# Deformable convolution with a routed expert FFN: expert results added onto an early-written output by the indirect DMA

## The chip, the cores and the metric

The kernel runs on one core of one Trainium2 chip. The metric is the device time of one execution in microseconds (us). The engines are PE (matmul), DVE (vector), ACT (activation), POOL (GpSimd), and SP, which issues most of the DMAs. Each engine has its own instruction queue, worked off in order, and they meet only at semaphores.

## The reference

The input is a batch of 4 images of 32x32 positions with 128 channels, 4,096 rows in all, in float32.

```python
x = x + conv(_ln_c(x), w_offset, b_offset, filt)      # 3x3 deformable convolution
t = _to_tokens(x)                                     # x1: 4,096 rows of 128
t = t + ffn(_ln_t(t), gate_w, gate_b, W1, b1, W2, b2)

# ffn, on rows xf
probs = softmax(xf @ gate_w + gate_b)                 # 8 experts
top2_vals, top2_idx = top_k(probs, 2)
cw = zeros.at[rows, top2_idx].add(top2_vals)
for e in range(8):
    y = gelu(xf @ W1[e] + b1[e]) @ W2[e] + b2[e]      # hidden width 256
    out = out + cw[:, e] * y
```

So every row goes through two of the eight experts, and its output is x1 plus the two results, each times its softmax share.

## The kernel before

**Bands.** The 4,096 rows are 32 bands of 128. The `step` functions of the engines run once per band in a loop of four bands per turn (`band_loop`, L305). Band b takes its sampling weights on PE (`spread_hats`, L1274), DVE (`multiply`, L918) and ACT (`copy_y`, L725), samples its window (`sample`, L1307, three groups), has ACT copy the samples out of PSUM (`evacuate_samples`, L755), and projects them with the filter (`project`, L1321). DVE then adds the projection to x1 (`residual`, L926), takes mean and variance, ACT takes the square root (`std_band`, L763) between the first and the second sample copy of the next band, and DVE takes the reciprocal and normalises (`normalise`, L941). PE computes the gate, DVE picks the two experts (`choose`, L955) and the row's place in each expert's region (`place_rows`, L985, four links). POOL packs the normalised row with its destination number (`pack`, L584) and scatters it with two indirect DMAs per band into the DRAM table `routed` (`scatter`, L596). `project` of a band waits for `place_rows` link 0 and for the sample copies; ACT's order of work within a band is fixed by its `step` (L790), DVE's by its own (L1093).

**Plan.** After the last band DVE counts the blocks of 256 rows per expert and writes a table `blk_i` of 39 blocks, in the order of experts (L1145 to L1168). SP and ACT fill the ends of the regions with padding rows. Blocks that are not needed (idle blocks, at the end of the 39) read a region of padding.

**Blocks.** Each of the 39 blocks uses one of four slots. SP reads the block's first row from `blk_i` into registers, copies the expert's weights (W1, b1, W2, b2) from the SBUF tensor `w_all` into the slot's `w_blk` (`load_weights`, L486), and loads 256 rows (`load_rows`, L492). PE transposes the rows, multiplies by W1, ACT applies Gelu, PE multiplies by W2 (`down`, L1437), DVE adds b2 (`finish`, L1194), and POOL writes the result rows with two indirect DMAs (`send`, L652) into the DRAM table `result`, a row's place there being its own number for its first expert and 4,096 further on for its second. Padding rows are dropped by the bounds check. DVE does not reuse a slot's `y` or `to` before the sends of the block four before have landed.

**Combination.** When all sends have landed (SP, L527), SP reads `result` back in groups of four bands, ACT multiplies one of the two results by its share (L846 to L852), DVE multiplies the other, adds x1 and adds both (L1213 to L1224), and SP stores the output. The shares are computed in one go after the plan (L1171 to L1180).

```python
652  def send(turn, place):
654      pool.wait_ge(s.y_done, i + 1)
655      pool.wait_ge(s.to_ready, i + 1)
657      for j in range(SUBS):
658          nc.gpsimd.indirect_dma_start(result, ..., y[:, slot, j, :], None, bounds_check=...)
```

Of the kernel before, what the change touches and what calls it, by code (L numbers as in the profile page):

```python
# [20 lines left out]
F32 = mybir.dt.float32  # L21
# [7 lines left out]
P = 128  # L29
# [18 lines left out]
ZERO_ROWS = 40  # L48
# [17 lines left out]
assert IDLE + BLOCK <= REGION  # L66
BLOCKS = (2 * P * BANDS + EXPERTS * (BLOCK - 1)) // BLOCK
ROW = C + 1

W_UP = HID + HALVES  # L70
WROW = W_UP + HALVES * C + C
RING = 4
SP_PADS = EXPERTS // 2
GB = 4
BACK = 4
# [13 lines left out]
def window_constants():  # L89
# [28 lines left out]
    for b in range(BANDS):  # L118
# [10 lines left out]
    token = np.arange(BANDS)[None, :, None] * P + p[:, None, None]  # L129
    dest = (token + np.arange(2) * (P * BANDS)).astype(np.int32)  # L130
    padding = np.zeros((P, SUBS, ROW), np.int32)
    padding[:, :, C] = 2 * P * BANDS + np.arange(SUBS) * P + p[:, None]
# [9 lines left out]
        "padding": padding,  # L142
    }


def program(nc, x_rows, x_tiles, w_offset, b_offset, filt, gate_w, gate_b, experts,
            rel, spread, fold, base, ident, before, table, dest, padding, out):
    with ExitStack() as ctx:
# [11 lines left out]
        result = nc.dram_tensor("result", [2 * P * BANDS + BLOCK, C], F32, kind="Internal").ap()  # L160
# [12 lines left out]
        dest_sb = sb("dest_sb", [P, BANDS, 2], I32)  # L173
# [20 lines left out]
        top_all = sb("top_all", [P, BANDS, EXPERTS])  # L194
# [23 lines left out]
        rs1 = sb("rs1", [P, 2])  # L218
        xn2 = sb("xn2", [P, 2, C])
# [30 lines left out]
        e_all = sb("e_all", [P, BANDS, EXPERTS])  # L250
        e_sum = sb("e_sum", [P, BANDS])
        share = sb("share", [P, 2, BANDS])
# [8 lines left out]
        blk_first = sb("blk_first", [1, BLOCKS])  # L261
        blk_row = sb("blk_row", [1, BLOCKS])
        blk_i = sb("blk_i", [1, BLOCKS], I32)
        pad_row = sb("pad_row", [1, EXPERTS], I32)


        w_blk = sb("w_blk", [P, RING, WROW])
# [5 lines left out]
        y_back = wide[:, 0:BACK * 2 * GB * C].rearrange("p (r c2 b c) -> p r c2 b c", r=BACK, c2=2, b=GB)  # L273
        res = sb("res", [P, BACK, GB, C])

# [4 lines left out]
        for name in (  # L280
# [7 lines left out]
            "route stashed place_psum place_ready placed_ready slot_f_ready slot_ready payload_ready scat_even scat_odd "  # L288
            "exp_in exp_out warmed share_step count_psum plan_step pad_ready plan_ready idle_written pads_written "
            "rows_in_0 rows_in_1 rows_in_2 rows_in_3 w_in_0 w_in_1 w_in_2 w_in_3 "  # L290
            "rowsT_psum rowsT_ready h_psum h_ready y_psum2 to_ready y_done "
            "sent_0 sent_1 sent_2 sent_3 back_0 back_1 back_2 back_3 scaled res_step res_ready "
            "stored_0 stored_1 stored_2 stored_3"
# [58 lines left out]
        back_arrived = (s.back_0, s.back_1, s.back_2, s.back_3)  # L352
        stored = (s.stored_0, s.stored_1, s.stored_2, s.stored_3)
# [26 lines left out]
        def _(sp):  # L380
# [75 lines left out]
            sp.dma_start(routed[IDLE_ROW:IDLE_ROW + BLOCK, :].rearrange("(j p) w -> p j w", p=P),  # L456
                         padding_sb[:, :, :].bitcast(F32)).then_inc(s.idle_written, 16)
# [4 lines left out]
            with sp.If(flag):  # L462
                pad_image()
                with sp.Fori(0, BANDS) as b:
                    sp.wait_ge(s.base_free, b + 1)
                    sp.dma_start(base_sb[:, :], base[b]).then_inc(s.base_loaded, 16)
            with sp.Else():
                for b in range(2, BPI):
                    load_windows(b, b % 2, 0, TILE * b)
                with sp.Fori(1, IMAGES) as m:  # L470
                    for r in range(BPI):
                        load_windows(m * BPI + r, r % 2, m, TILE * r)

# [5 lines left out]
            def first_rows(turn, place, n):  # L479
# [3 lines left out]
                    min_val=0, max_val=IDLE_ROW)  # L483
                return rows

            def load_weights(turn, place, row):  # L486
                i, slot, uses = block_at(turn, place)
                expert = nc.s_assert_within(row >> REGION_BITS, 0, EXPERTS - 1)
                at_least(sp, s.y_done, i - (RING - 1))
# [20 lines left out]
            sp.wait_ge(s.plan_ready, 1)  # L510
# [15 lines left out]
            for slot in range(RING):  # L526
                sp.wait_ge(sent[slot], 16 * SUBS * (TURNS + (slot < REST)))  # L527
            back = result[0:2 * P * BANDS, :].rearrange("(c g b p) d -> c g p b d", c=2, b=GB, p=P)
            out_v = out.rearrange("(g b) p c -> g p b c", b=GB)

            def load_back(g):
                for c2 in range(2):
                    sp.dma_start(y_back[:, g % BACK, c2], back[c2, g]).then_inc(back_arrived[g % BACK], 16)

            for g in range(BACK):
                load_back(g)
            for g in range(BANDS // GB):
                sp.wait_ge(s.res_ready, g + 1)
                sp.dma_start(out_v[g], res[:, g % BACK, :, :]).then_inc(stored[g % BACK], 16)
                if g + BACK < BANDS // GB:  # L540
                    load_back(g + BACK)
            for slot in range(BACK):
                sp.wait_ge(stored[slot], 16 * (BANDS // GB // BACK))
# [3 lines left out]
        def _(pool):  # L547
# [10 lines left out]

            pool.wait_ge(s.early_loaded, 16 * N_EARLY)
# [937 lines left out]
```

## Time and profile before

| what | us |
|---|---|
| three runs | 402.12, 403.15, 404.54 |
| median | 403.15 |
| span of the profiled execution | 400.06 |
| median less span | 3.1 |
| PE busy, share of the span | 315.2, 79% |
| POOL busy | 228.9, 57% |
| DVE busy | 227.3, 57% |
| ACT busy | 195.6, 49% |

The profile gives the span of its execution, from the first instruction to the last; its time around the span is not measured by itself, so the difference to the median stands for it. Busy shares are means over stages with different limits, so the stages have to be read one by one: 0 to 45 us the first normalisation and the offsets, 45 to 250 the bands, 250 to 274 the plan and the first loads, 274 to 375 the blocks, 375 to 400 the combination. L numbers are lines of the kernel before. An entry such as "[0.88 <-DVE slot L1007]" is the engine's idle time before the instruction and what ended it. SPq, ACTq, POOLq and DVEq are the engines' queues with their register, wait and DMA-issuing instructions.

### The profile page before, as it was taken

The numbers are of one execution on the slowest core, as the hardware profiler recorded it, in microseconds if no ns is written. First come the engines' busy times: TensorE is split into PE (matmuls) and PEld (weight loads), VectorE is DVE, ScalarE is ACT, GpSimd is POOL, SyncE is SP. The second block draws the span as 40 slices with busy tenths as digits, with TensorE's granted clock in tenths as the row PEclk, the third lists the DMA queues.
The fourth block names the chain that finished last, engine by engine and source line by source line (L and its number), as shares of the span: only waits on it lengthen the run. The fifth ranks groups of instructions, "written<-read, shape, count | busy, mean of one in ns | idle before, by whom it ended". The sixth has DMA issues, their size and how long they took to land.

```text
span 400.1 us, 9901 instructions
## 1 busy us (share of the span) xinstructions
PE 315.2 (79%) x2395; PEld 264.9 (66%) x2395; DVE 227.3 (57%) x988; ACT 195.6 (49%) x526; POOL 228.9 (57%) x351
## 2 busy tenths in 40 slices
PE   0999799999999999999999995049989797885000
PEld 0354688888889888898898994038867686774000
DVE  3983257878778787787887876502222122332085
ACT  1253566565565665756656652314444444442063
POOL 4013043777777777777777766204777777777300
PEclk9999899999999999999999999558999999999555
DMA  8958612222222222222222220855777777762298
GB/s 209 274 164 249 265 54 75 89 80 100 78 93 85 82 99 78 90 94 76 98 84 83 95 80 26 145 139 169 223 222 243 230 231 232 227 221 72 82 315 234
DMA packets 52450, 57.88 MB, mean 145 GB/s; under 512 B 6892, under 2 KB 40423, under 8 KB 52424
## 3 DMA queue, kind: packets, MB, share of 16 engines
q1 hardware_dynamic: 45031, 48.16, 39.1%
q0 software_dynamic: 4544, 8.44, 6.6%
q10 hardware_dynamic: 2848, 0.99, 1.4%
q8 instruction: 9, 0.15, 0.2%
q14 instruction: 18, 0.14, 0.1%
HBM read 30.70 MB, written 14.97 MB: 114 GB/s over the span
## 4 chain that ended last, share of the span: by engine, by line
PE 53%; SPq 16%; issue 10%; DMA 6%; ACT 4%; DVE 4%; POOL 2%; ACTq 2%; DVEq 1%; POOLq 0%
PE bank L1326 18%; PE bank L1315 15%; SPq L481 5%; PE bank L1248 5%; SPq L490 4%; SPq L496 3%; DMA wide<-result 2%; PE bank L1279 2%; PE bank L1433 2%; ACT samp L758 2%; PE bank L1269 2%; PE bank L1260 2%; POOL result L658 2%; DMA routed<-padding_sb 1%; DMA result<-y,to 1%
## 5 line engine op out<-in xcount | busy, mean ns | idle before, releaser
L658 POOL DMA_INDIRECT result<-y,to x78 | 76.8, 985 | 43.8 <-DVE to L1191 26.8
L1326 PE MATMUL bank<-filt_sb,samp 128*128 128x128 f32 x576 | 79.3, 283 | 4.1 <-ACT samp L758 2.5
L1326 PEld LDWEIGHTS bank<-filt_sb,samp 128*128 128x128 f32 x576 | 69.1, 191 | 18.1 <-ACT samp L758 14.2
L1315 PE MATMUL bank<-S,xwin 100*128 100x144 f32 x512 | 78.9, 298 | 1.8 <-issue 1.7
L602 POOL DMA_INDIRECT routed<-payload,slot x64 | 63.2, 987 | 18.5 <-issue 13.5
L758 ACT ACTIVATE samp<-bank 128x432 f32<-128x432 f32 (+1 forms) x96 | 46.3, 484 | 52.8 <-PE bank L1315 52.8
L1315 PEld LDWEIGHTS bank<-S,xwin 100*128 100x128 f32 x512 | 67.7, 193 | 2.2 <-issue 2.0
L923 DVE TENSOR_TENSOR S<-ysp,bank 100x512 f32<-100x512 f32 (+1 forms) x96 | 52.5, 550 | 22.9 <-ACT ysp L729 21.8
L1433 PE MATMUL bank<-rowsT,w_blk 128*128 128x256 f32 x156 | 44.4, 408 | 13.3 <-DMA w_blk<-w_all 10.2
L1199 DVE TENSOR_TENSOR y<-bank,w_blk 128x256 f32<-128x256 f32 x39 | 16.6, 425 | 66.0 <-PE bank L1442 64.2
L822 ACT ACTIVATE rowsT<-bank 128x256 f32<-128x256 f32 x39 | 15.0, 384 | 61.0 <-PE bank L1424 61.0
L729 ACT ACTIVATE ysp<-bank 100x512 f32<-100x512 f32 (+1 forms) x96 | 43.6, 494 | 2.4 <-PE bank L1279 1.5
L579 POOL TENSOR_TENSOR rest<-hat 128x180 f32<-128x180 f32 x32 | 17.0, 531 | 47.2 <-ACT hat L715 47.2
L1442 PE MATMUL bank<-w_blk,hid 128*128 128x128 f32 x312 | 42.1, 279 | 0.0
L1433 PEld LDWEIGHTS bank<-rowsT,w_blk 128*128 128x128 f32 x156 | 27.5, 197 | 20.0 <-ACT hid L829 8.0
L1442 PEld LDWEIGHTS bank<-w_blk,hid 128*128 128x128 f32 x312 | 38.8, 195 | 0.3 <-ACT hid L829 0.2
L829 ACT ACTIVATE hid<-bank,w_blk 128x256 f32<-128x256 f32 x78 | 32.6, 473 | 0.6 <-PE bank L1433 0.6
L1279 PE MATMUL bank<-hatT,spread_sb 120*100 120x512 bf16 (+1 forms) x96 | 32.0, 333 | 0.1
L1282 PE MATMUL bank<-hatT,spread_sb 120*100 120x512 bf16 (+1 forms) x96 | 31.2, 325 | 0.8 <-DVE S L923 0.8
L1424 PE MATMUL bank<-ident_sb,rows_in 128*128 128x128 f32 x78 | 15.9, 287 | 15.1 <-DMA rows_in<-routed 15.1
L570 POOL TENSOR_TENSOR dist<-offs,rel_sb 128x180 f32<-128x180 f32 x32 | 16.2, 508 | 19.3 <-issue 10.7
L1424 PEld LDWEIGHTS bank<-ident_sb,rows_in 128*128 128x128 f32 x78 | 11.0, 147 | 20.3 <-DMA rows_in<-routed 15.1
(110 smaller groups left out, 493.1 us busy)
## 6 DMA issues: line engine op xcount, KB each, us to landing
w_blk<-w_all SPq DMA_DIRECT2D x39, 321.0 KB
xwin<-lines SPq DMA_DIRECT2D x64, 120.0 KB
xwin<-lines SPq DMA_DIRECT2D x32, 160.0 KB
rows_in<-routed SPq DMA_DIRECT2D x39, 129.0 KB
wide<-result SPq DMA_DIRECT2D x16, 256.0 KB, 4.8
w_all<-in_experts SPq DMA_DIRECT2D x4, 642.0 KB, 7.4
out_tiles<-res SPq DMA_DIRECT2D x8, 256.0 KB, 4.6
wide<-in_x_rows SPq DMA_DIRECT2D x3, 512.0 KB, 8.6
```

Source lines behind the costliest of these rows:

```text
L602: nc.gpsimd.indirect_dma_start(routed, bass.IndirectOffsetOnAxis(slot[:, par, c2:c2 + 1], 0), payload[:, par, c2, :], None).then_inc((s.sc ...
L658: nc.gpsimd.indirect_dma_start(result, bass.IndirectOffsetOnAxis(to[:, slot, j:j + 1].bitcast(U32), 0), y[:, slot, j, :], None, bounds_che ...
L729: nc.scalar.activation(ysp[:, slot, 0:n], bank[slot][0:Q, 0:n], ACT.Copy).then_inc(s.y_ready, 1)
L758: nc.scalar.activation(sample_view(par, g), bank[5 + (par + g) % 2][:, 0:GROUPS[g] * TAPS * TT].rearrange("c (t k p) -> c t k p", k=TAPS, ...
L829: nc.scalar.activation(hid[:, slot, h, :], bank[RING + slot][:, h * BLOCK:(h + 1) * BLOCK], ACT.Gelu, bias=w_blk[:, slot, HID + h:HID + h ...
L923: nc.vector.tensor_tensor(S[:, par, c0:c0 + n], ysp[:, slot, 0:n], bank[2 + slot][0:Q, 0:n], ALU.mult).then_inc(s.S_ready, 1)
L1279: nc.tensor.matmul(bank[slot][0:Q, 0:n], spread_sb[:, 2 * odd, :], moving, start=True, stop=True).then_inc(s.y_psum, 1)
L1282: nc.tensor.matmul(bank[2 + slot][0:Q, 0:n], spread_sb[:, 2 * odd + 1, :], moving, start=True, stop=True).then_inc(s.x_psum, 1)
L1315: last = nc.tensor.matmul(bank[5 + (par + g) % 2][:, i * TAPS * TT:(i + 1) * TAPS * TT], xwin[:, par, t, :], weights[:, t], start=True, st ...
L1326: last = nc.tensor.matmul(bank[7][:, 0:C], samp[:, par, j, :], filt_sb[:, order[j], :], start=(j == 0), stop=(j == TAPS - 1))
L1433: last = nc.tensor.matmul(bank[RING + slot][:, h * BLOCK:(h + 1) * BLOCK], w_blk[:, slot, h * P:(h + 1) * P], rowsT[:, slot, :], start=Tru ...
L1442: last = nc.tensor.matmul(bank[slot][:, BLOCK + j * C:BLOCK + (j + 1) * C], hid[:, slot, h, j * P:(j + 1) * P], w_blk[:, slot, W_UP + h * ...
```

## The change

The table `result` and the combination are gone. The output tensor itself is the target of the sends, which add their rows to what lies there (an indirect DMA with an add). The output holds x1 before that: SP stores each band's x1 into it during the bands. A row's two results come from two experts, so POOL lets no block start before all blocks of earlier experts have landed. Results are scaled by their share before they are sent; the share travels with the row, computed per band, and rows grow from 129 to 130 words. Padding and idle blocks are added to spare rows of the output, which POOL zeroes at the start. The square root and reciprocal become Ln and Exp on ACT. W2 is no longer copied into the slot: PE reads it from `w_all` at an address from a register.

```diff
 # SP, per band
+            def begin_out(b):
+                at_least(sp, s.x1_ready, b + 1)
+                settle(sp)
+                sp.dma_start(out[bass.ds(b * P, P), :], x1[:, b, :]).then_inc(s.out_begun, 16)
-            sp.dma_start(routed[IDLE_ROW:IDLE_ROW + BLOCK, :].rearrange("(j p) w -> p j w", p=P),
-                         padding_sb[:, :, :].bitcast(F32)).then_inc(s.idle_written, 16)
+            sp.dma_start(routed[IDLE_ROW:LAST_ROW + BLOCK, :], idle.bitcast(F32)).then_inc(s.idle_written, 16)
 # SP, per block
-                sp.dma_start(w_blk[:, slot, :], w_all[:, expert, :]).then_inc(w_arrived[slot], 16)
+                sp.dma_start(w_blk[:, slot, :], w_all[:, expert, 0:W_KEPT]).then_inc(w_arrived[slot], 16)
             def load_rows(turn, place, row):
+                at_least(sp, s.y_done, (i - (RING - 1)) * SUBS)
 # POOL, at the start
+            for n in range(RING):
+                nc.gpsimd.dma_start(out[TRASH + n * part:TRASH + (n + 1) * part, :].rearrange(
+                    "(p r) c -> p (r c)", p=P), zero[:, 0:part * C // P]).then_inc(sent[n], 16)
 # POOL, per block
+            def send(turn, place, ahead):
+                for other in range(RING):
+                    pool.wait_ge(sent[other], ((ahead + (RING - 1 - other)) >> 2) * (16 * SUBS) + 16)
                 pool.wait_ge(s.to_ready, i + 1)
                 settle(pool)
                 for j in range(SUBS):
+                    pool.wait_ge(s.y_done, i * SUBS + (j + 1))
+                    settle(pool)
                     nc.gpsimd.indirect_dma_start(
-                        result, ..., y[:, slot, j, :], None, bounds_check=2 * P * BANDS - 1, oob_is_err=False
+                        out, ..., y[:, slot, j, :], None, compute_op=ALU.add).then_inc(sent[slot], 16)
 # ACT, per band
             def std_band(b, par):
                 act.wait_ge(s.mean1_ready, b + 1)
-                nc.scalar.activation(sd1[:, par:par + 1], mv1[:, par, 1:2], ACT.Sqrt,
-                                     bias=eps_t[:, :]).then_inc(s.std1_ready, 1)
+                nc.scalar.activation(sd1[:, par:par + 1], mv1[:, par, 1:2], ACT.Ln,
+                                     bias=eps_t[:, :]).then_inc(s.ln_ready, 1)
+                act.wait_ge(s.ln_ready, b + 1)
+                at_least(act, s.xn2_ready, b - 1)
+                nc.scalar.activation(rs1[:, par:par + 1], sd1[:, par:par + 1], ACT.Exp, scale=-0.5
+                                     ).then_inc(s.std1_ready, 1)
+            def exp_top(b, par):
+                act.wait_ge(s.ntop_ready, b + 1)
+                at_least(act, s.share_ready, b - 1)
+                nc.scalar.activation(e_top[:, par, :], top[:, par, :], ACT.Exp, bias=ntop[:, par:par + 1],
+                                     accum_out=e_sum[:, par:par + 1]).then_inc(s.e_ready, 1)
 # ACT step: exp_top(b - 3) between evacuate_tokens(b - 2) and copy_y(b, 2)
 # DVE, per band
-                nc.vector.reciprocal(rs1[:, par:par + 1], sd1[:, par:par + 1]).then_inc(s.dve_rstd, 1)
-                    nc.vector.tensor_copy(top_all[:, b, :], top[:, par, :]).then_inc(s.stashed, 1)
+                    nc.vector.tensor_scalar(ntop[:, par:par + 1], top[:, par, 0:1], -1.0, None, ALU.mult
+                                            ).then_inc(s.ntop_ready, 1)
+                elif link == 4:
+                    dve.wait_ge(s.e_ready, b + 1)
+                    nc.vector.reciprocal(e_inv[:, par:par + 1], e_sum[:, par:par + 1]).then_inc(s.inv_ready, 1)
+                else:
+                    dve.wait_ge(s.inv_ready, b + 1)
+                    nc.vector.tensor_scalar(payload[:, par, :, C + 1], e_top[:, par, 0:2], e_inv[:, par:par + 1], None,
+                                            ALU.mult).then_inc(s.share_ready, 1)
 # DVE step: link 4 of band b - 3 after residual(b - 1) link 0, link 5 after hats(b + 2) link 0
 # DVE, per block, after the addition of b2
+                dve.wait_ge(s.y_sum, i + 1)
+                for j in range(SUBS):
+                    nc.vector.tensor_scalar(y[:, slot, j, :], y[:, slot, j, :], rows_in[:, slot, j, C + 1:C + 2], None,
+                                            ALU.mult).then_inc(s.y_done, 1)
 # PE, per block
-                                                w_blk[:, slot, W_UP + h * C:W_UP + (h + 1) * C],
+                                                w_all[:, expert, W_KEPT + h * C:W_KEPT + (h + 1) * C],
...
 # removed: load_back, res, y_back, share and the three combination loops of SP, ACT and DVE
```

## Rows read from the trace of the kernel before

**Rows 1.** Busy time by stage: start:end, length, busy (instructions) per engine, clock, DMA.
```profile
core 0: us, PE busy (x) PEld busy (x) DVE busy (x) ACT busy (x) POOL busy (x), PEclk, DMA share, GB/s
58.00:238.00 180.00, 175.82 (x1465) 156.33 (x1464) 143.19 (x665) 110.50 (x291) 129.41 (x226) 1.00 0.26 87
274.00:375.00 101.00, 79.02 (x518) 68.56 (x516) 24.94 (x75) 40.98 (x110) 76.81 (x78) 0.97 0.64 200
```

**Rows 2.** Timeline of POOL, block stage (start, duration; first two and last of 78).
```profile
274.23 0.99 POOL L658 DMA_INDIRECT result<-y,to  x1 [20.37 <-DVE to L1191]
275.52 0.99 POOL L658 DMA_INDIRECT result<-y,to  x1 [0.30 <-DVE to L1191]
...
373.52 0.98 POOL L658 DMA_INDIRECT result<-y,to  x1 [0.30 <-issue]
```

**Rows 3.** The sends' line (durations min/median/max in ns), and waits of 265 to 376.
```profile
L658 POOL DMA_INDIRECT result<-y,to x78: 982/984/995, 274.2 to 373.5; - x78
...
DVE to L1191 <- DMA result<-y,to: 9.7, 20, 1.3
```

**Rows 4.** Chain that ended last (start, duration): two landings of sends, and the end.
```profile
360.63 3.35 DMA result<-y,to
...
373.52 2.12 DMA result<-y,to
...
396.58 0.69 DVE res L1223
```

**Rows 5.** Timeline at the end of the bands: a POOL queue that had run empty.
```profile
250.41 0.31 DVE L1007 CAST slot<-slot_f 128x2 uint32<-128x2 f32 x1
...
251.63 0.96 POOL L602 DMA_INDIRECT routed<-payload,slot  x1 [0.88 <-DVE slot L1007]
```

**Rows 6.** Timeline of one band, ACT with the two ends of its chain.
```profile
160.06 0.53 ACT L758 ACTIVATE samp<-bank 128x432 f32<-128x432 f32 x1 [1.64 <-PE bank L1315]
161.13 0.17 DVE L939 BATCH_NORM_AGGREGATE mv<-st 128x2 f32<-128x6 f32 x1
161.33 0.29 ACT L765 ACTIVATE sd<-mv,eps_t 128x1 f32<-128x1 f32 x1
161.53 0.51 ACT L758 ACTIVATE samp<-bank 128x432 f32<-128x432 f32 x1
162.19 0.40 ACT L758 ACTIVATE samp<-bank 128x288 f32<-128x288 f32 x1
```

**Rows 7.** Chain that ended last, two bands on.
```profile
162.64 1.38 PE bank L1326 x10
...
167.51 0.30 ACT sd L765
...
168.63 0.18 DVE place L991
...
168.89 1.38 PE bank L1326 x10
```

**Rows 8.** Waits in the bands, 58 to 238 (total, times, longest); SP's of the span.
```profile
POOL rest L579 <- ACT hat L715: 34.5, 28, 3.8
...
PEld bank L1326 <- ACT samp L758: 13.2, 23, 0.7
...
SPq L414 <- PE bank L1315: 103.1, 30, 4.7
```

**Rows 9.** SP's line of the weight copies in the block stage.
```profile
L490 SPq DMA_DIRECT2D w_blk<-w_all x39: 495/507/602, 257.6 to 358.7; - x39
```

**Rows 10.** Timeline of the first 20 us.
```profile
11.31 1.63 DVE L864 BATCH_NORM_STATS2 st<-wide 128x6 f32<-128x128 f32 x8
...
17.14 0.52 POOL L561 CAST spread_sb<-spread_f 120x400 bf16<-120x400 f32 x1 [12.49 <-DMA gb_sb<-in_gate_b]
```

**Rows 11.** Chain that ended last, between the bands and the blocks.
```profile
256.13 5.79 DMA routed<-padding_sb
262.17 2.27 DMA rows_in<-routed
```

More of the change, by code:

```diff
@@ L142, in window_constants @@
         "padding": padding,
+        "idle": idle,
     }
 def program(nc, x_rows, x_tiles, w_offset, b_offset, filt, gate_w, gate_b, experts,
-            rel, spread, fold, base, ident, before, table, dest, padding, out):
+            rel, spread, fold, base, ident, before, table, dest, padding, idle, out):
     with ExitStack() as ctx:
@@ L472, in _ @@
                         load_windows(m * BPI + r, r % 2, m, TILE * r)
+                        begin_out(m * BPI + (r - 3))
+                for b in range(BANDS - 3, BANDS):
+                    begin_out(b)
             sp.wait_ge(s.pad_ready, 1)
@@ L526, in _ @@
             for slot in range(RING):
[L527 to L543, printed above, removed]
+                sp.wait_ge(sent[slot], 16 + 16 * SUBS * (TURNS + (slot < REST)))
         @block.gpsimd
@@ L650, in _, with blocks_ahead @@
                 scatter(BANDS - 1, 1)
-            def send(turn, place):
+            pool.wait_ge(s.plan_ready, 2)
+            pool.wait_ge(s.out_begun, 16 * BANDS)
+            for n in range(RING):
+                pool.wait_ge(sent[n], 16)
+            def blocks_ahead(turn, place, n):
+                _, values = nc.values_load_multi_w_load_instructions(
+                    blk_ahead[0:1, bass.ds(turn * RING + place, n)], engines=[mybir.EngineType.Pool],
+                    min_val=0, max_val=BLOCKS)
+                return values
+            def send(turn, place, ahead):
                 i, slot, uses = block_at(turn, place)
-                pool.wait_ge(s.y_done, i + 1)
+                for other in range(RING):
+                    pool.wait_ge(sent[other], ((ahead + (RING - 1 - other)) >> 2) * (16 * SUBS) + 16)
                 pool.wait_ge(s.to_ready, i + 1)
@@ L796, in step @@
                         evacuate_tokens(b - 2, par)
+                    if not known or b >= 3:
+                        exp_top(b - 3, 1 - par)
                     if not known or b >= 1:
@@ L1187, in keep_dest @@
                     settle(dve)
[L1188 removed]
+                sent_before(slot, uses)
                 if not isinstance(i, int):
@@ L1435, in up, with experts_of, down @@
                 last.then_inc(s.h_psum, 1)
-            def down(turn, place):
+            def experts_of(first, n):
+                _, rows = nc.values_load_multi_w_load_instructions(
+                    blk_i[0:1, bass.ds(first, n)], engines=[mybir.EngineType.PE],
+                    min_val=0, max_val=LAST_ROW)
+                return [nc.s_assert_within(row >> REGION_BITS, 0, EXPERTS - 1) for row in rows]
+            def down(turn, place, expert):
                 i, slot, uses = block_at(turn, place)
```

209 lines of the change are left out of this document (103 added, 106 removed).

## The prediction

> **What bounds the kernel now.** I read busy time by stage first, then the timeline of the engine that looks saturated in each stage, then the chain that ended last.
>
> Blocks: POOL is 76.8 us busy in 101 us, PE 79.0 [rows 1]. The shares hide who paces. POOL's timeline shows it: the 78 sends start every 1.29 us, 0.98 us each and 0.30 us apart, from 274.23 to 373.52 without one larger gap [rows 2], so the stage is 78 x 1.29 = 100.5 us of POOL. DVE confirms it: 20 times it waits 9.7 us in all for landed sends [rows 3]. SP comes close: its 39 weight copies go from 257.6 to 358.7 [rows 9], 2.66 us apart with the wait for the first rows among them, against POOL's 2.58 per block.
>
> Bands: PE is busy 175.8 of 180 us [rows 1], but busy here includes pipelined overlap. The next band's projection waits for ACT's last sample copy: 23 times, 13.2 us of weight-load idling [rows 8]. ACT's chain in one band runs without a hole: first sample copy at 160.06, square root at 161.33, second copy 161.53, last copy 162.19 [rows 6], projection at 162.64 [rows 7]. The square root begins as soon as DVE's variance is there (161.13 + 0.17 = 161.30 [rows 6]). Every fourth band goes by DVE instead: square root 167.51, `place` 168.63, projection 168.89 [rows 7]. So ACT and DVE set the band's period of about 6.2 us jointly with PE.
>
> Combination: the last send lands at 373.52 + 2.12 = 375.64 [rows 4], and the span ends at 400.06; 24.4 us are reading back, scaling, adding and storing.
>
> **The change part by part**, against the profiled span of 400.06 us; the median of the runs is 3.1 us above it, and I carry these along.
>
> *Combination removed.* 24.4 us go. SP still has to see the last sends land; 0.4 us for that is my estimate: 24.0 saved. The last sends belong to idle blocks. Today their rows are dropped, landing in 2.12 us; a send with rows takes 3.35 [rows 4]. They now carry rows: +1.2.
>
> *Sends.* The number stays 78. How long POOL takes for a send with an add no row shows. Nearest is the same instruction without it, 982 to 995 ns over all 78, the emptied ones included [rows 3]: POOL's time does not follow what leaves. I take no change. Ends: below, 78 x 0.03 us = 2 us gained, because the bounds check goes and a scatter without one takes 0.96 [rows 5]; above, half as much again, 78 x 0.49 = 38 us. The landing could grow by a read of the destination: 0 to 2.3 us, a row load's whole way [rows 11]; I take 0, since the sends land like a plain scatter in the nearest row.
>
> *New wait on earlier experts.* Seven times in 39 blocks the expert changes and POOL waits until everything sent has landed. The queue is in order: the next send, the register loads and everything behind stand still. From a send's start to its landing 3.35 us [rows 4]; from a released wait to the start of a send on an empty POOL queue 0.9 us (250.72 to 251.63 [rows 5]); less the 1.29 us pitch [rows 2], 3.0 us each. POOL is the bound, so nothing covers it: 7 x 3.0 = +21. Low end: restart hidden, 7 x 2.1 = 14; high end: a read leg added, 7 x 5.3 = 37. What waits behind POOL is DVE (`y`, `to`), then PE and SP, which all have the time. POOL's register work for the four waits lies beside its send, 0.98 us of each 1.29 [rows 2]; exposed, it would show as a longer pitch.
>
> *DVE's scaling* (two small operations per block after b2) lies beside POOL's pitch; DVE is 24.9 of 101 us busy [rows 1]. Only the first block pays it, about 0.4 us.
>
> *W2 in place, smaller copies, PE's register loads.* Weight copies shrink from 321 to 193 KB. Since POOL paces, I cost them at nothing either way; the cover is POOL's 2.58 us per block plus 21 us of stalls. If POOL were faster, SP [rows 9] would be next. The new wait in `load_rows` comes one place ahead of one that `load_weights` already had: nothing.
>
> *Bands, ACT.* `std_band` costs 0.20 us of ACT now (161.33 to 161.53 [rows 6]). Ln must finish (0.29), the wait releases (0.04), Exp takes another 0.20: 0.53, so +0.33 on the chain that releases the projection. `exp_top` stands before a hole of 1.64 us in which ACT waits for samples [rows 6]: hidden.
>
> *Bands, DVE.* Two small operations (links 4, 5), each with a wait, and a wait in `choose`, stand between the residual and the variance; the copy of `top` and `ntop` swap evenly. In a queue where such an operation takes 0.1 to 0.2 us, the variance comes about 0.2 us later, and Ln with it. The removed reciprocal lies behind Exp and shortens only the `place` path. Together 0.33 + 0.22 = 0.55 us on 31 bands: +17. Ends: 0, if PE's own work covers it (its idle is 4 us in 180 [rows 1]); and 1.0 per band, 31 us, if each wait costs 0.1 more.
>
> *Bands, the rest.* SP's store of x1 needs some 0.5 us of a queue that waits 103 us for samples [rows 8]; POOL's extra wait stands in a queue that waits 34.5 us for ACT [rows 8]. Nothing; without that cover SP would lose 0.5 us per band.
>
> *Start.* POOL zeroes 1 MB by four DMAs while the images load. DVE takes up the second image at 11.31 [rows 10]; a delay of that image would show there. POOL itself is idle until 17.14 [rows 10]. The larger idle table (0.9 MB) moves while the offsets are computed. +0.5, ends 0 and 3.
>
> *Between bands and blocks.* Two more links before the count, +0.4, the reciprocal of the last band, -0.2, the first scaling +0.4. The longer plan lies beside the padding rows, which land 5.79 us after their issue at 256.13 [rows 11]. +0.6.
>
> Sum: 400.06 - 24.0 + 1.2 + 21 + 17 + 0.5 + 0.6 = 416.4, with 3.1 around it **419.5 us**.
>
> **Rivals.**
>
> *The bands pay nothing (faster).* Place: ACT between the first and last sample copy. PE is 97.7% busy there; if its period is its own, the 0.55 us vanish under it, and the missing reciprocal may shorten the `place` bands (0.2 us in 8 bands, -1.6). Then 419.5 - 17 - 1.6 = 401, with 394 if the stalls are at their low end as well. It decides at a band period that stays at or below 6.2 us. Against it: the 13.2 us that PE's weight loads wait for ACT [rows 8], and the projection that follows the last copy at once.
>
> *The add costs POOL or the DMA engines more (slower).* Every send longer by up to 0.49 us: 438 at half of that, 457 in full. For it: nothing in this trace adds on the way. Against it: the emptied sends take POOL as long as full ones [rows 3]. The Trainium skill (Collectives: The Full Stack, Why ReduceScatter is half of AllGather) says that an add in the DMA engines needs two source reads, two read descriptors per chunk where a copy has one. No row shows it; by that rule this rival is the one that happens.
>
> *The tables do not stay (slower).* Were Ln and Exp to reload ACT's table each time, every band would pay over 2 us, some 480. The change asks for one set ahead of the bands; little speaks for it.
>
> **How the numbers follow.** The forecast case has 0.54, with a narrow own range of 408 to 430. The bands that pay nothing 0.2, the dearer add 0.22, the tables 0.04. A measurement of this kernel can tell about 0.5%, 401.1 to 405.2. Faster: 0.11 from the first rival and 0.06 from the forecast case with all its low ends together: 0.17. Same: 0.05 and 0.02: 0.07. Slower takes the rest, 0.76. The range goes from 397, between the low rival's ends, to 448, inside the dearer add; below it some 0.08 and above it some 0.11 are left.
>
> **What would show it.** The combination's 24 us gone, the last landing near the end. In POOL's timeline seven gaps of about 4.3 us between the starts of neighbouring sends, the rest still at 1.29. A band period of 6.7 instead of 6.2, with Ln and Exp 0.33 us apart and the variance later. I am wrong if the pitch of sends inside an expert is not 1.29, if the gaps are far from 3 us above it, or if the band period does not move.

## The result, and the profile after

The changed kernel takes 463.11 us (462.13 to 464.9, 4 runs) against 403.38 us (402.12 to 404.54, 4 runs): 1.149 times as long, 95% interval 1.146 to 1.153. The forecast was 419.5 with a range up to 448. The sign was right, the size was not. The profiled execution took 463.29 us with a span of 461.5, so the two spans, 400.06 and 461.5, differ by 61.4 us. The time around the span is 1.8 to 2.0 us in every execution whose span is on record; the 3.1 us that stood for it before the change is larger because the execution profiled there was shorter than the median. One execution of the kernel before, 1119.59 us beside f5 and f6, was a slow one and is left out below.

Windows of the changed kernel, the two stages of [rows 1] (bands, then blocks):

```profile
core 0: us, PE busy (x) PEld busy (x) DVE busy (x) ACT busy (x) POOL busy (x), PEclk, DMA share, GB/s
62.00:255.00 193.00, 179.39 (x1466) 158.10 (x1465) 145.17 (x692) 124.10 (x378) 131.16 (x227) 1.00 0.28 91
292.00:457.00 165.00, 100.64 (x521) 82.84 (x519) 41.34 (x151) 40.97 (x110) 121.14 (x78) 0.79 0.58 101
```

The blocks went from 101 to 165 us. POOL still issues 78 sends there, but they keep it busy for 121.14 us in place of 76.81. The sends' line, answering [rows 3] (ns, minimum, median, maximum; then what ended the idle time before them and who waited):

```profile
L679 POOL DMA_INDIRECT out_tiles<-y,to x78: 1544/1552/1610, 292.1 to 454.7; - x78
its engine sat idle before it (us, times) until:
  issue: 23.8, 51
...
  DVE to L1225: 52.7, 22
```

One send costs POOL 1.55 us with the add, 0.98 without. DVE, which waited 9.7 us for landed sends before, now waits 52.7: everything stands behind POOL. POOL's timeline, answering [rows 2]: the first sends, four of the seven restarts after a wait for earlier experts, and the last.

```profile
292.05 1.61 POOL L679 DMA_INDIRECT out_tiles<-y,to  x1 [20.39 <-DVE to L1225]
293.97 1.57 POOL L679 DMA_INDIRECT out_tiles<-y,to  x1 [0.30 <-issue]
...
305.77 1.55 POOL L679 DMA_INDIRECT out_tiles<-y,to  x1 [2.79 <-issue]
...
402.97 1.55 POOL L679 DMA_INDIRECT out_tiles<-y,to  x1 [3.65 <-DVE y L1237]
...
431.71 1.55 POOL L679 DMA_INDIRECT out_tiles<-y,to  x1 [3.06 <-DVE y L1237]
...
441.72 1.55 POOL L679 DMA_INDIRECT out_tiles<-y,to  x1 [2.89 <-DVE y L1237]
...
454.71 1.55 POOL L679 DMA_INDIRECT out_tiles<-y,to  x1 [0.30 <-issue]
```

Inside an expert the pitch is 1.857 us, of which 0.30 is the old gap. Seven gaps are larger: 2.79, 3.23, 3.18, 2.94, 3.65, 3.06, 2.89, together 19.6 us above seven ordinary ones. So the stage, from the first send's start to the last one's end, is 164.2 us against 100.3: 78 x 0.568 = 44.3 for the longer sends and 19.6 for the gaps make the 63.9.

The chain in one band, answering [rows 6]:

```profile
158.10 0.53 ACT L778 ACTIVATE samp<-bank 128x432 f32<-128x432 f32 x1 [1.64 <-PE bank L1337]
...
159.26 0.29 ACT L785 ACTIVATE sd<-mv,eps_t 128x1 f32<-128x1 f32 x1
159.59 0.20 ACT L789 ACTIVATE rs<-sd 128x1 f32<-128x1 f32 x1
159.69 0.51 ACT L778 ACTIVATE samp<-bank 128x432 f32<-128x432 f32 x1
...
160.35 0.40 ACT L778 ACTIVATE samp<-bank 128x288 f32<-128x288 f32 x1
```

Ln and Exp start 0.33 us apart. From Ln's start to the next sample copy it is 0.43 us, where the square root left 0.20. The two ends of the bands are the first and the last projection:

```profile
55.81 0.94 PE L1348 MATMUL bank<-filt_sb,samp 128*128 128x128 f32 x6 [1.56 <-ACT samp L778]
...
258.83 0.94 PE L1348 MATMUL bank<-filt_sb,samp 128*128 128x128 f32 x6
```

Before, these stood at 51.88 and 241.71. So the start lost 3.9 us and the 31 band periods 13.2 (203.02 against 189.83, or 0.43 each). Each is a difference of two profiles, and profiles scatter: the first projection lies between 51.88 and 54.09 in the five kernels here with the old start, and between 53.89 and 56.03 in the eleven with the new one; the 31 periods take 189.8 to 190.7 us in the four kernels whose bands are as before, and 202.8 to 204.5 in the eleven that have the changed bands. From the last projection to the first send it is 33.2 us against 32.5. After the last send's end 5.2 us are left against 25.55. What they wait for is on record in the drains, the last that each queue does before the engines meet at the end (in the kernel before, then in the changed one; ns, start in us):

```profile
L148 POOLq DRAIN  x1: 13807/13807/13807, 367.3 to 367.3; - x1
```

```profile
L153 POOLq DRAIN  x1: 12367/12367/12367, 448.9 to 448.9; - x1
L153 SPq COMPARE_BRANCH  x1: 38/38/38, 458.1 to 458.1; - x1
L153 SPq DRAIN  x1: 13/13/13, 458.3 to 458.3; - x1
```

SP has seen all sends land at 458.1 and is done at 458.3, but POOL's drain ends only at 461.3, and the span ends at 461.5. In the kernel before POOL's drain ended at 381.1, beside the combination.

| stage | forecast | measured |
|---|---|---|
| start | +0.5 | +3.9 |
| bands | +17 | +13.2 |
| between bands and blocks | +0.6 | +0.7 |
| the sends' own length | 0 | +44.3 |
| seven waits for earlier experts | +21 | +19.6 |
| combination and last landing | -22.8 | -20.3 |
| sum | +16.3 | +61.4 |

### The profile page after: what moved, and what is told of

It is laid out like the page before. It is cut to its first block, busy times and chain, and to the rows that moved or that the text cites. A ratio compares the mean times of both kernels' runs of the same rounds, so it can differ in the third digit from the quotient of the medians.

```text
span 461.5 us, 10816 instructions
## 1 busy us (share of the span) xinstructions
PE 342.4 (74%) x2395; PEld 281.5 (61%) x2396; DVE 231.6 (50%) x1056; ACT 198.6 (43%) x587; POOL 276.9 (60%) x356
## 3 DMA queue, kind: packets, MB, share of 16 engines
q0 software_dynamic: 13600, 10.43, 15.8%
## 4 chain that ended last, share of the span: by engine, by line
PE 26%; issue 22%; DMA 12%; DVE 11%; ACT 10%; POOL 7%; SPq 3%; ACTq 3%; POOLq 2%; DVEq 1%
PE bank L1348 10%; DMA out_tiles<-y,to 9%; POOL out_tiles L679 6%; PE bank L1270 4%; ACT samp L778 3%; PE bank L1471 2%; PE bank L1455 2%; ACT sd L785 2%; DMA w_blk<-w_all 2%; PE bank L1337 2%; PE bank L1282 1%; ACT hat L735 1%; DMA rows_in<-routed 1%; ACT e_top L795 1%; PE bank L1258 1%
## 5 line engine op out<-in xcount | busy, mean ns | idle before, releaser
L679 POOL DMA_INDIRECT out_tiles<-y,to x78 | 121.1, 1553 | 63.5 <-issue 23.8
L607 POOL DMA_INDIRECT routed<-payload,slot x64 | 63.1, 986 | 20.3 <-issue 14.1
L1455 PE MATMUL bank<-rowsT,w_blk 128*128 128x256 f32 x156 | 52.5, 470 | 13.4 <-DMA w_blk<-w_all 11.0
L1471 PE MATMUL bank<-w_all,hid 128*128 x312 | 51.9, 320 | 0.1
L1446 PE MATMUL bank<-ident_sb,rows_in 128*128 128x128 f32 x78 | 19.2, 334 | 42.5 <-DMA rows_in<-routed 21.6
L1471 PEld LDWEIGHTS bank<-w_all,hid 128*128 128x128 f32 x312 | 47.7, 233 | 0.8 <-issue 0.3
L1455 PEld LDWEIGHTS bank<-rowsT,w_blk 128*128 128x128 f32 x156 | 33.6, 239 | 20.2 <-issue 11.2
L1225 DVE COPY to<-rows_in 128x2 int32<-128x2 int32 x39 | 6.5, 167 | 60.9 <-DMA out_tiles<-y,to 52.7
L868 ACT ACTIVATE hid<-bank,w_blk 128x256 f32<-128x256 f32 x78 | 32.5, 473 | 0.6 <-PE bank L1455 0.6
```

The lines of the kernel that those rows point to most:

```text
L607: nc.gpsimd.indirect_dma_start(routed, bass.IndirectOffsetOnAxis(slot[:, par, c2:c2 + 1], 0), payload[:, par, c2, :], None).then_inc((s.sc ...
L679: nc.gpsimd.indirect_dma_start(out, bass.IndirectOffsetOnAxis(to[:, slot, j:j + 1].bitcast(U32), 0), y[:, slot, j, :], None, compute_op=AL ...
L868: nc.scalar.activation(hid[:, slot, h, :], bank[RING + slot][:, h * BLOCK:(h + 1) * BLOCK], ACT.Gelu, bias=w_blk[:, slot, HID + h:HID + h ...
L1455: last = nc.tensor.matmul(bank[RING + slot][:, h * BLOCK:(h + 1) * BLOCK], w_blk[:, slot, h * P:(h + 1) * P], rowsT[:, slot, :], start=Tru ...
L1471: last = nc.tensor.matmul(bank[slot][:, BLOCK + j * C:BLOCK + (j + 1) * C], hid[:, slot, h, j * P:(j + 1) * P], w_all[:, expert, W_KEPT + ...
```

## The experiments

Where an edit drops the sum, its time still reads as that of the rest. The column "sends" is from the first send's start to the last one's in the profiled execution; it is the measure of the block stage.

| run | sends, us | time, us | before beside it |
|---|---|---|---|
| kernel before | 99.3 | 403.38 | |
| changed kernel | 162.7 | 463.11 | 403.38 |
| e1_plain | 143.7 | 445.91 | 402.54 |
| e2_no_order | 146.0 | 447.76 | 402.54 |
| e3_plain_no_order | 143.2 | 443.85 | 402.54 |
| f1_w2_back | 163.9 | 463.99 | 403.48 |
| f2_plain_w2_back | 123.1 | 423.59 | 403.48 |
| f3_plain_no_order_w2_back | 109.6 | 410.61 | 403.48 |
| f5_no_pool_loads | 107.9 | 408.18 | 403.16 |
| f7_share_kept | 99.4 | 400.64 | 402.81 |
| f4_before_w2 | 113.6 | 416.97 | 403.48 |
| f6_pe_loads | 119.6 | 424.52 | 403.16 |
| h1_skip (72 sends) | 91.5 | 395.68 | 402.77 |

**The add and the order, one at a time and together.** e1 overwrites in place of adding:

```diff
-                        None, compute_op=ALU.add).then_inc(sent[slot], 16)
+                        None).then_inc(sent[slot], 16)
```

> The changed kernel, its sends without the add: each row overwrites its output row, so the output holds one expert's scaled result in place of the sum; the waits on earlier experts stay. Theory (the add itself makes POOL's time per send longer): a send takes 0.98 us again in place of 1.55, the pitch goes from 1.86 to 1.29 us, 78 x 0.57 = 44 us go, some 419 us; the seven gaps stay. Rival (the pitch is set by what POOL does beside the add, its register loads and four waits per block, or by the target in the output tensor): the pitch stays at 1.86 and the time at about 463.

e2 keeps the add and takes away what the wait is for: a token's second result goes to an output half of its own, padding rows are dropped at the bounds, x1 is stored to both halves.

```diff
-                for other in range(RING):
-                    pool.wait_ge(sent[other], ((ahead + (RING - 1 - other)) >> 2) * (16 * SUBS) + 16)
...
-                        None, compute_op=ALU.add).then_inc(sent[slot], 16)
+                        None, bounds_check=TRASH - 1, oob_is_err=False, compute_op=ALU.add).then_inc(sent[slot], 16)
```

> The changed kernel with its adds, each of a token's two results added onto an output half of its own (x1 is stored into both halves, rows of padding are dropped at the bounds), so that no send waits on earlier experts; the output lacks the second result. Theory (gaps and pitch are independent): the seven gaps go, 463 - 20 = 443 us, and the pitch stays at 1.86. Rival (POOL's longer pitch comes from draining, a queue that is emptied and restarted): the pitch falls too and the time goes below 430.

e3 is e2 without `compute_op`.

> Both at once: halves of their own without the waits, and no add; the output lacks the combination. Theory: both savings add up, 463 - 44 - 20 = 399 us, the pitch is that of the kernel before, 1.29. Rival (another engine or SP's queue becomes the bound first, since the weight copies now come later or W2 is read in place): it stays above 405.

Measured: 445.91, 447.76 and 443.85 us. The send's price came out as the theory has it. The sends' line of e1:

```profile
L679 POOL DMA_INDIRECT out_tiles<-y,to x78: 952/958/994, 293.1 to 436.9; - x78
```

But e1 saves 17 us where 44 were expected, e2 saves 15 of 20, and both edits together little more than one: 443.85 where 399 was expected. In e2 POOL still paces: its pitch stays at 1.86 as its theory says, and of the seven gaps three shorter ones are left, 3.0 us in all above ordinary ones. In e1 and e3 the sends no longer stand close (22 and 19 gaps of over 0.4 us). The theory of independent terms falls; e3's rival holds, there is a second bound near 143 us of sends. In e3 the chain that ended last shows it, once per turn of four blocks (start, duration):

```profile
293.77 2.23 DMA w_blk<-w_all
...
296.22 1.12 PE bank L1455 x4
297.35 2.59 issue
...
300.62 1.71 PE bank L1471 x8
302.33 1.71 PE bank L1455 x4
...
306.35 0.37 DVE y L1237
...
306.90 0.38 SPq L511
...
308.73 2.21 DMA w_blk<-w_all
```

From one weight copy at this place to the next it is 14.96 us, 3.74 per block. In it PE stands still for 2.59 us after a block's first product, where `experts_of` reads four values into registers, and the products behind the pause are slow. Behind them SP's row load (L511) follows DVE's scaling (L1237). Two suspects: PE's register loads that W2 in place needs, and SP's new wait ahead of a block's rows.

**W2 back in the block's weights.** f1 undoes W2 in place in the changed kernel, f2 also the add, f3 also the order (on e3).

```diff
-                sp.dma_start(w_blk[:, slot, :], w_all[:, expert, 0:W_KEPT]).then_inc(w_arrived[slot], 16)
+                sp.dma_start(w_blk[:, slot, :], w_all[:, expert, :]).then_inc(w_arrived[slot], 16)
...
-                                                w_all[:, expert, W_KEPT + h * C:W_KEPT + (h + 1) * C],
+                                                w_blk[:, slot, W_KEPT + h * C:W_KEPT + (h + 1) * C],
...
-                        experts = [None] + experts_of(0, n - 1) if begun else experts_of(turn * RING - 1, n)
+                        experts = [None] * n
```

> The changed kernel with W2 copied into each block's weights as before the change (full copies, PE reads no registers); adds and waits on earlier experts stay. Theory (POOL paces the changed kernel: 78 x 1.86 us plus seven drains, and PE's pauses of 2.6 us per four blocks lie under it): no change, 463 us within 3. Rival (PE's pauses cost time in the changed kernel as well): 440 to 455.

> W2 copied as before and the sends without the add; the waits on earlier experts stay; the output lacks the sum. Theory (W2 in place is the second bound: PE stands 2.6 us per four blocks for its register loads, which stretches the loop over weights, products and the next weight copy to 14.9 us per four blocks): with it gone POOL paces again at 1.29 us, 463 - 44 = 419 us. Rival (the second bound is SP's new wait ahead of a block's rows, for the scaled results of an earlier block): it stays near 444.

> W2 copied as before, no add, and halves of their own without waits on earlier experts; the output lacks the combination. Theory (W2 in place is the second bound): 463 - 44 - 20 = 399 us, sends 1.29 us apart throughout. Rival (SP's wait ahead of the rows): about 441, as with W2 in place.

Measured: 463.99, 423.59 and 410.61. f1 does not move, so in the changed kernel POOL alone paces. f2 against f1 is the add alone, with W2 copied: 40.4 us, near the 44 that its 78 longer sends come to. f2 against e1 is 22 us: with a cheap send W2 in place is the bound. f2 is 4.6 us and f3 11.6 above the expectation; something remains.

**W2 in place alone, on the kernel before.** f4 adds only that; f6 adds only PE's register loads, with W2 copied and read as before.

```diff
# f4 and f6, PE, once per turn of four blocks (cut)
+                    if place == 0:
+                        experts = [None] + experts_of(0, n - 1) if begun else experts_of(turn * RING - 1, n)
# f6 against f4: W2 is copied as before, and the products read the copy
-                                                w_all[:, expert, W_KEPT + h * C:W_KEPT + (h + 1) * C],
+                                                w_blk[:, slot, W_UP + h * C:W_UP + (h + 1) * C],
```

> The kernel before with W2 read in place and the smaller weight copies alone. Theory (PE's register loads bound the blocks at 14.9 us per four): the sends' stage grows from 99 to about 143 us, some 445 us. Rival (as predicted: under POOL's 2.58 us per block it costs nothing): 403 us.

> The kernel before with PE's register loads alone: four values per four blocks, which no product uses; W2 is copied and read as before. Theory (PE's pause for the loads, and the half clock that follows it, make the whole price of W2 in place): as with W2 in place, 417 us. Rival (the price lies in reading W2 out of the one large tile, or in the smaller copies): 403 to 405.

Measured: 416.97 (+13.5, not +42) and 424.52 (+21.4). f4's number was missed: neither W2 in place alone (f4, 113.6) nor all the rest without it (f3, 109.6) brings the sends to the 143 us of e3. Both lie in the loop shown above and together do more than their sum, 44 us against 14 and 10; no run takes SP's wait alone out of e3, so why they do more is open. f6 shows that the loads alone are enough for the price; f4 is some 7 us below it, and whether its smaller copies or the reading in place do that was not separated. PE's queue in f6:

```profile
L1439 PEldq TENSOR_LOAD <-blk_i x11: 314/1510/2037, 266.5 to 387.5; - x11
```

One load of the four values takes 1.5 us, and PE idles around it. The Trainium skill (DMA: Bandwidth & Descriptors, Latency and other measured facts) gives such a load a floor of about 0.6 us; here the median is 2.5 times that, while the smallest, 0.31, the last load, of one value, lies below it, so the figure is no floor in this trace. The eight pauses for four values are 2.6 to 3.3 us long in f6, 22.6 in all, about the 20.3 us by which its sends' stage grew; the pauses themselves are enough for f6's price.

Behind a pause the products can be slow as well. In f4 this is one (PE's timeline, then windows; the clock is the last but two):

```profile
330.89 0.69 PE L1425 MATMUL bank<-ident_sb,rows_in 128*128 128x128 f32 x2 [2.32 <-issue]
331.37 1.92 PE L1450 MATMUL bank<-w_all,hid 128*128 x8
...
337.83 1.06 PE L1450 MATMUL bank<-w_all,hid 128*128 x8
```

```profile
331.00:333.30 2.30, 2.30 (x11) 2.29 (x12) 0.00 (x0) 1.11 (x3) 0.00 (x0) 0.50 0.11 33
337.00:342.00 5.00, 4.73 (x32) 3.99 (x30) 1.52 (x6) 2.22 (x6) 2.95 (x3) 1.00 0.53 163
```

Behind this pause the granted clock is 0.50, the lower of the two levels, 1.2 GHz, and a block's eight products with W2 take 1.92 us; from 337 it is 1.00, and they take 1.06. It is not so behind every pause: of f4's eight pauses for four values two are followed by such slow products (1.92 and 1.76, the others 1.15 or 1.16), in e3 all eight (1.92 to 2.07). The mean clock of the sends' stage is 0.93 in f4 and 0.83 in e3. So the lower clock goes the same way as the 44 us of e3; how much of them it makes was not measured.

**The rest of f3.** f5 takes POOL's four register loads per turn away (nothing uses them in f3); f7 in addition copies the share beside the target row when a block's rows are taken up, so that SP's row loads need not wait for the scaled results.

```diff
# f5
-                for place, ahead in enumerate(blocks_ahead(turn, 0, RING)):
-                    send(turn, place, ahead)
+                for place in range(RING):
+                    send(turn, place, 0)
# f7
-                at_least(sp, s.y_done, (i - (RING - 1)) * SUBS)
...
-            nc.vector.tensor_scalar(y[:, slot, j, :], y[:, slot, j, :], rows_in[:, slot, j, C + 1:C + 2], None,
+            nc.vector.tensor_scalar(y[:, slot, j, :], y[:, slot, j, :], to[:, slot, j, 1:2].bitcast(F32), None,
```

> The kernel with W2 copied, no add and halves of their own, now also without POOL's four register loads per turn of four blocks (nothing uses them there); the output lacks the combination. Theory (POOL's register loads stand openly at a pitch of 1.29 us: some 0.7 us at each turn and what follows from it, 10 us in all): 410.6 - 10 = 401 us, sends 1.29 us apart throughout. Rival (the gaps come from SP's later row loads, behind the scaled results): 408 to 411.

> As the kernel without POOL's register loads, and with the share copied beside the target row when a block's rows are taken up, so that SP's row loads wait for the targets alone, as before the change, and no longer for the scaled results; the output lacks the combination. Theory (SP's wait for scaled results, 13.7 us in 20 waits, makes the rows late and is the rest of the stage's 8.5 us over the kernel before): the sends stand 1.29 us apart throughout, 408 - 8 = 400 us. Rival (the longer way from product to send by the two scalings does it): 406 to 409.

Measured: 408.18 (405.43 to 409.87) and 400.64. f5's rival holds: the gap of about 1.0 us that stood at eight of the nine turns went, but SP still waited in 20 places, and gaps of up to 3.0 us stood at DVE's `y`. SP's waits in the sends' stage of f5, and then of f7:

```profile
SPq L511 <- DVE y L1237: 13.7, 20, 2.3
```

```profile
SPq L504 <- DVE y L1232: 0.2, 1, 0.2
```

With that wait gone the sends of f7 run 99.4 us for 78, as in the kernel before, scalings and all. The prediction had called this wait "nothing".

**What the price of a send goes by.** g1 sends, by the place in the turn, 64 rows with add, 64 without, 128 rows of 64 columns with add, and 128 full rows with add.

```diff
+                    if place == 0:
+                        nc.gpsimd.indirect_dma_start(out, bass.IndirectOffsetOnAxis(to[0:64, slot, j:j + 1].bitcast(U32), 0),
+                            y[0:64, slot, j, 0:C], None, compute_op=ALU.add).then_inc(sent[slot], 16)
...
```

> The changed kernel with four kinds of sends, by the block's place in its turn: 64 rows with add, 64 rows without, 128 rows of 64 columns with add (into a tensor of its own), 128 rows of 128 columns with add as it was; the output lacks half the rows of two places and all of the third. Theory (POOL's price goes by row, with or without add, and the add makes each row dearer): about 0.85 us for 64 rows with add, 0.6 without, and 1.55 for half the columns. Rival (by byte): half the columns cost as half the rows. Rival (a fixed price per instruction with add): all three adds near 1.55.

Groups of POOL's lines in g1, which ran once (count, busy us, mean ns), the four kinds as L681, L684, L687, L690:

```profile
L687 POOL DMA_INDIRECT halfrows<-y,to x20 | 31.9, 1595 | 8.4 <-issue 7.8 <-DMA out_tiles<-y,to 0.6
L681 POOL DMA_INDIRECT out_tiles<-y,to x20 | 28.5, 1427 | 25.4 <-DVE to L1235 19.9 <-issue 4.0 <-DMA out_tiles<-y,to 1.2
L690 POOL DMA_INDIRECT out_tiles<-y,to x18 | 28.1, 1562 | 16.9 <-DVE y L1247 6.6 <-DVE to L1235 6.2 <-issue 4.1
L684 POOL DMA_INDIRECT out_tiles<-y,to x20 | 18.4, 922 | 15.2 <-issue 13.7 <-DMA out_tiles<-y,to 1.2 <-DVE y L1247 0.3
```

The theory falls, the last rival holds: the price is nearly all per instruction. Half the rows save 0.13 us of 1.56 with add, and half the columns save nothing. Without add, 64 rows take 0.92 against the 0.96 of 128 rows in e1. In the sizes tried the add costs 0.5 to 0.6 us a piece.

**Bands and start.** e4 is the kernel before with Ln and Exp for square root and reciprocal; e5 is the changed kernel with DVE's two share links moved from ahead of the variance to around the normalisation.

```diff
# e5, DVE step
-                    place_rows(b - 3, other, 4)
                     choose(b - 2, par, 0)
                     hats(b + 2, par, 0)
-                    place_rows(b - 3, other, 5)
...
+                    place_rows(b - 3, other, 4)
                     normalise(b - 1, other)
+                    place_rows(b - 3, other, 5)
```

> The kernel before with the one edit on ACT's chain alone: the square root and DVE's reciprocal become Ln and Exp, the second waiting for the first. Theory as predicted (0.33 us on the chain that releases the projection, in 31 bands): +10, some 413 us. Rival (ACT's part is hidden, and the band's 0.43 us come from DVE's two added links ahead of the variance): within 2 us of the kernel before, 403.

> The changed kernel with DVE's two share links moved from ahead of the variance to around the normalisation. Theory (of the 13.2 us that the bands lost, Ln and Exp make 8.3, and the two links ahead of the variance the other 5, 0.16 us per band): the period falls from about 6.65 to 6.5 us, some 458 us. Rival (the rest of the 13 us comes from elsewhere, the stores of x1 or the longer Exp with its sum): 463, the period as it was.

Measured: 410.79 (1.0209 of before, 1.0184 to 1.0234) and 461.38. In e4's trace the projections run from 52.45 to 251.03, 198.58 us against 189.83: Ln and Exp make 8.75 of the 13.2 us. In e5 they run from 55.48 to 256.47, 200.99 against 203.02: the links' place ahead of the variance makes 2.0 of the 5 expected, little more than profiles of the same bands scatter (1.7). The last 2.4 us were not separated.

e7b issues the four zeroing transfers in POOL's fourth step and the idle table's behind the first image's windows.

```diff
# POOL: the zeroing loop moved
+                    if known and b == HEAD - 1:
+                        zero_trash()
# SP: behind begin_out(b - 3) of the first image
+                sp.dma_start(routed[IDLE_ROW:LAST_ROW + BLOCK, :], idle.bitcast(F32)).then_inc(s.idle_written, 16)
```

> The changed kernel with the four zeroing transfers issued behind the third band and the idle table's transfer behind the first image's windows. Theory (the first projection's 3.9 us of delay come from these 2 MB beside the first loads): the first projection starts at about 52.5 us in place of 55.8, some 460 us. Rival (the delay is one of instructions, at the start and at the branch): 463, projection at 55.8.

Measured: 460.58. The first projection is back:

```profile
51.98 1.28 PE L1354 MATMUL bank<-filt_sb,samp 128*128 128x128 f32 x10
```

So these transfers, with the instructions that issue them, make most of the start's 3.9 us, within the scatter of some 2 us between profiles. The bands run from 51.98 to 255.79, as long as before within the scatter. That the transfers delay the first loads is not the whole of it. POOL's first instruction behind the branch that every engine takes ahead of the bands, on a flag `far` that DVE works out, in the kernel before and in the changed one:

```profile
49.59 0.50 POOL L570 TENSOR_TENSOR dist<-offs,rel_sb 128x180 f32<-128x180 f32 x1 [10.73 <-issue]
```

```profile
53.52 0.51 POOL L572 TENSOR_TENSOR dist<-offs,rel_sb 128x180 f32<-128x180 f32 x1 [12.79 <-issue]
```

DVE has `far` ready at 45.5 in the kernel before and at 47.4 in the changed one, 1.9 us later; from there to POOL's instruction it is 4.1 us before, 6.1 in the changed kernel and 3.5 in e7b. So about half of the loss stands behind the branch, where the profile shows no wait, and e7b does not tell the transfers from their instructions.

**A kernel faster than both.** If a send costs POOL the same whether it moves rows or not [rows 3], the sends of idle blocks are worth taking out. h1 puts the last three blocks of the kernel before under a branch on every engine, on a flag that DVE works out with the plan.

```diff
-            for place in range(REST):
-                send(TURNS, place)
+            with pool.If(rest_pool):
+                for place in range(REST):
+                    send(TURNS, place)
```

> The kernel before, with the last three blocks under a branch on every engine that is taken only if one of them has rows (here none has). Theory (in the kernel before POOL's price per send is the whole of the stage, idle blocks included): 6 x 1.29 = 7.7 us less a branch of 1 to 2 us, some 397 us. Rival (the branch and the register loads on PE eat it): 402 to 404.

Measured: 395.68 us (395.4 to 396.99, 5 runs), 0.983 of the kernel before, interval 0.981 to 0.985. Its line of sends:

```profile
L663 POOL DMA_INDIRECT result<-y,to x72: 982/983/994, 276.9 to 368.3; - x72
```

72 sends of the old length, 7.8 us less of them in the stage; the medians fall by 7.1, so by them the branch cost under 1 us. The gain holds for inputs that leave these blocks empty.

## Why the prediction was wrong, by its own steps

- **The failed step is "Sends: I take no change."** It measured +44.3 us, and the upper end given, 38, was too low as well: 0.57 us per send against 0.49. The argument was that an emptied send takes POOL as long as a full one, so POOL's time does not follow what leaves. That observation is right, and g1 nearly repeats it. What does not follow is that the kind of operation is free: the price is nearly all per instruction, and the add has a higher one. The rival of the dearer add, at 0.22, is the one that happened. The Trainium skill (Collectives: The Full Stack, Why ReduceScatter is half of AllGather) spoke for it with two read descriptors for an add; the trace agrees in direction, and not in the figure: POOL's queue moved the same 10.43 MB in 4864 packets in e1 and 13600 in the changed kernel, and what the time went by was POOL's own instruction. Why the add costs POOL more no run shows.
- **Waits on earlier experts**: +21 forecast, +19.6 measured on the timeline, 16.7 of it saved by e2. The mechanism is right, seven gaps; that the size came so near is in part luck. From send to send over a wait it was 4.66 us in the mean against 4.25 in the forecast, and the pitch to take off was 1.86 and not 1.29.
- **Smaller copies, W2 in place, PE's registers: "nothing either way."** A second failed step, hidden by the first. The sentence is true of the changed kernel (f1), but for another reason than the one given. The cover was named as POOL's 2.58 us per block. Under that cover they are not hidden: f4 +13.5 us, f6 +21.4. They are hidden under 3.71 us per block, the price of the add. With the add at the price that I gave it, the time would have been e1's 446, not 419.5; with both steps undone it is f2's 423.59.
- **"The new wait in `load_rows`: nothing."** The same: hidden in the changed kernel, 7.5 us where the rest is cheap (f5 to f7). The wait stood one place ahead of an old one in SP's queue, but it took a place of lead from the rows.
- **POOL's register work beside its send**: right at a pitch of 1.86, where no gap at a turn is larger; at 1.29 eight of nine turns showed one of about 1.0 us (f3).
- **Bands**: +17 forecast, +13.2 measured. ACT's part is 8.75 of a forecast 10; DVE's links ahead of the variance make 2.0 of 7. The rival of the tables did not happen: ACT loads a table four times in the changed kernel, five times in the kernel before.
- **Start**: +0.5 forecast, +3.9 measured, at the upper end of 3 or above it, given the scatter. The 2 MB of zeros and idle rows, or the instructions that issue them, do cost time at the start (e7b), half of it only behind the branch.
- **Combination**: -22.8 forecast, -20.3 measured. The send starting at 454.71 has landed by 458.1, so some 3.4 us to the end of the span are left where I had put 0.4. They are POOL's drain, which the forecast left out: it ends 5.0 us after the last send's end. In the kernel before it took 6.6 and lay beside the combination.
- **Between bands and blocks**: +0.6 and +0.7.

Without the add, the order and W2 in place, and with the two small repairs, the change is worth 2 us (f7: 400.64, 0.993 of before, interval 0.990 to 0.996, with the sum left out). What was removed, 20 us, pays for the bands and the start, 17 us, and leaves little.

## What to carry to other kernels

Price an operation that no row shows as an instruction of a new kind, not as its nearest relative, above all on the engine that paces: there every tenth is multiplied by the count. Where an edit is costed at nothing because something covers it, check it against the cover that is left if that something is as cheap as hoped; three edits here hid under a cost that I had put at zero. And when two edits each save little and both together no more, look for a second bound before looking for an error.

## What the runs showed that I had not expected

- An indirect DMA with an add takes POOL 1.55 us per instruction, without 0.96 to 0.98; half the rows cost 1.43 and 0.92.
- A load of four register values on PE took 1.25 to 1.5 us in the median and stopped PE for 2.3 to 3.3. Eight products behind some of these pauses took 1.92 us, at a granted clock of 0.50, and 1.06 later at 1.00.
- An added send lands 3.3 us after POOL's instruction starts, in the median; the same send without the add lands after 2.2 (e1). POOL's longer instruction is 0.6 of these 1.1 us, so the way behind it grew by some 0.5. The sends' lines of the changed kernel and of e1:

```profile
DMA to landing us min/median/max: 3.2/3.3/4.4
```

```profile
DMA to landing us min/median/max: 2.2/2.2/3.3
```

- POOL's drain ended 5.0 us after the last send's end in the changed kernel and 6.6 in the kernel before. It shows as soon as nothing longer stands behind the sends.
